# Macaron block with attention: the value product's four column groups become four quarters of the queries, one burst per key block

## The chip, the cores and the metric

The kernel runs on one core of one Trainium2 chip. The metric is the device time of one execution in microseconds. Engines: TensorE (PE), VectorE (DVE), ScalarE (ACT), GpSimd (POOL) and SyncE (SP), which issues all DMAs here.

## The reference

Input x is (4, 1024, 128) in f32. Three sublayers, each with a layernorm in front:

```
x = x + 0.5 * ffn(layernorm(x))      # 8 experts, top 2, hidden 256
x = x + attention(layernorm(x))      # 16 heads of 8, rotary, softmax over 1024 keys, out projection
x = x + 0.5 * ffn(layernorm(x))      # same weights as the first
```

With four batches and 16 heads there are 64 (batch, head) pairs, called heads 0 to 63 here. For each, attention computes softmax(q k / sqrt(8)) v for 1024 queries and 1024 keys. The key stack holds the f32 values split into bf16 parts, so the score product has 48 rows; three more rows subtract the maximum of each query.

## The kernel before

**Stages.** The first FFN takes chunks of 512 tokens (NCH = 8) and computes q, k and v behind them. Then come the 64 heads. The second FFN takes the 8 chunks again; each chunk's attention is normalised, projected and added one chunk ahead of it (`norm_attention`, `out_projection`, `add_attention`). PE, ACT, DVE, POOL and SP each run an instruction stream of their own, in program order, tied together by semaphores. Heads 4 to 59 are a hardware loop of 14 rounds of four heads, in which a wait's count comes from a register; heads 0 to 3 and 60 to 63 are written out.

**One head.** It has 8 key blocks of 128 keys. A score tile is 128 keys by 512 queries, so a head has 16 tiles (HALVES), i = 2 kb + j. Per i, PE issues in this order (`head`, L934):

- `key_scores` (L900, matmul L907): 51 rows, 512 columns, bf16, into one of three score banks (`score`, SCORE_BANKS = 3). It waits until the exp three places before has read that bank (`bank_free`). PE's place 7 in this rotation (MT_AT) is a transposition of the maxima of the next head (`max_transpose`, L897), which takes a bank for itself.
- `max_scores` (L869, matmul L878): 48 rows, for the head after the next; two of them make a tile of 128 queries by 1024 keys, on which DVE takes a maximum (L1252). Two such tiles are buffered. Q and K of heads two apart lie in different halves of the partitions.
- at every fourth i (3, 7, 11, 15), `weigh_values` (L910, matmul L921): the value product of a pair of key blocks, in f32, with the exponentials as the moving operand. Four matmuls fill four column groups of 32 in the array, hence four groups of 32 partitions of one PSUM bank (`opsum`): (even block, first 512 queries), (even, second), (odd, first), (odd, second). In the trace each of these matmuls is two, a first and a second pass. A value tile has 8 columns of v and columns of ones, which give the denominator. The pair weighed is the one before: at i = 3 the last pair of the previous head, at i = 7 the first of this one.

ACT does the 16 exponentials of a head (L675) into `probs`, 8 slots of 1024 columns. After exp 3 it copies the previous head's `opsum` to `ot` (`o_copy`, L657 to L663), and before exp 7 it copies the transposed maxima to `mrow` (L655). `weigh_values` of the first pair of a head waits for this `ot` (`ot_ready`). POOL splits the maxima into three bf16 parts and copies the head's values to `vh` (`v_head`). SP loads q and k of the head three further on, stores `ot` to the DRAM tensor `o_parts`, and loads `mrow` into Q (`head`, L381).

**After the heads.** `o_parts` holds, for each head and each half of the queries, two partial sums (even and odd key blocks). For a chunk SP loads both denominators (`load_den`), DVE adds and inverts them (`invert_denominator`), SP stores the result and loads both partial sums and the inverse, spread over the 8 rows of a head (`load_att`); POOL adds the two partial sums (`sum_attention`, L533), DVE multiplies (`norm_attention`, L1125).

Of the kernel before, what the change touches and what calls it, by code (L numbers as in the profile page):

```python
# [22 lines left out]
F32 = mybir.dt.float32  # L23
# [8 lines left out]
P = 128  # L32
# [22 lines left out]
HALF = 64  # L55
PAIRS = KB // 2
VW = 32
PIECE = H * CH // P
QSLOTS = 4
PSLOTS = 8  # L60
HALVES = 2 * KB
# [12 lines left out]
def at_least(eng, sem, count):  # L74

    if isinstance(count, int) and count <= 0:
        return
    eng.wait_ge(sem, count)  # L78
# [49 lines left out]
def build(nc, x_in, qkv_w, qkv_b, v_b, out_w, out_b, wr_t, w1_in, w2_t, cos_t, sin_t, out):  # L128
    q_stack = nc.dram_tensor("q_stack", (NH, STACK, T), BF16).ap()
    k_stack = nc.dram_tensor("k_stack", (NH, STACK, T), BF16).ap()  # L130
    rdens = nc.dram_tensor("rdens", (NCH, H, CH), F32).ap()
    o_parts = nc.dram_tensor("o_parts", (NH, P, CH), F32).ap()
    with ExitStack() as ctx:
        def sb(name, shape, dt=F32):
            return ctx.enter_context(nc.sbuf_tensor(name, shape, dt))

        def sem(name):
            return ctx.enter_context(nc.semaphore(name))
# [68 lines left out]
        mrow = sb("mrow", [PARTS * KB, 2, P], BF16)  # L207
        ot = sb("ot", [P, 2, CH])
        att = sb("att", [P, 2, 2, CH])
        att_sum = sb("att_sum", [P, CH])  # L210
        den = sb("den", [P, 2, PIECE])
        den_sum = sb("den_sum", [P, PIECE])
        rden_thin = sb("rden_thin", [P, PIECE])
# [18 lines left out]
        mpsum = ps[0:PARTS * KB, MT_BANK, 0:P // 2].bitcast(BF16)  # L232
        opsum = ps[:, 7, :]

# [58 lines left out]
        den_loaded = sem("den_loaded")  # L293
        den_summed = sem("den_summed")
        att_summed = sem("att_summed")
        den_inverted = sem("den_inverted")
# [17 lines left out]
        def _(sp):  # L314
# [34 lines left out]
            def load_head(r, u):  # L349
                n = QSLOTS * r + u  # L350

                at_least(sp, probs_used, PAIRS * (n - QSLOTS + 1))
                for tile, stack in ((Q, q_stack), (K, k_stack)):
                    sp.dma_start(tile[u][0:STACK, :],
                                 stack[bass.ds(n, 1)].rearrange("n s t -> (n s) t")).then_inc(head_loaded[u], 16)
# [36 lines left out]
            def load_den(r, u):  # L392
                c = CPB * r + u
                at_least(sp, den_inverted, c)
                for a in range(2):
                    src = o_parts[bass.ds(r * H, H), 32 * (2 * a + u) + HD, :].rearrange("h (s q) -> h s q", q=PIECE)
                    sp.dma_start(den[:, a, :], src).then_inc(den_loaded, 16)


            def load_att(r, u):  # L400
                c = CPB * r + u
                sp.wait_ge(den_inverted, c + 1)
                sp.dma_start(rdens[bass.ds(c, 1)].rearrange("c h (s q) -> (c h s) q", q=PIECE),
                             rden_thin[:]).then_inc(rden_stored, 16)

                at_least(sp, attn_ready, c - 1)
                alone(sp)
                sp.wait_ge(rden_stored, 16 * (c + 1))
                for a in range(2):
                    at = 32 * (2 * a + u)  # L410
                    sp.dma_start(att[:, u, a, :], o_parts[bass.ds(r * H, H), at:at + HD, :]).then_inc(att_loaded[u], 16)
                thin = rdens[bass.ds(c, 1)].rearrange("c h q -> (c h) q").unsqueeze(1).to_broadcast((H, HD, CH))
                sp.dma_start(rden[:, u, :], thin).then_inc(att_loaded[u], 16)

# [46 lines left out]
        def _(pool):  # L461
# [50 lines left out]
            def v_head(r, u):  # L512
                n = QSLOTS * r + u

                at_least(pool, probs_used, PAIRS * (n - 1))
                alone(pool)
                nc.gpsimd.tensor_copy(vh[:, u % 2, :, 0:HD],
                                      V[:].rearrange("p b h k d -> p (b h) k d")[:, bass.ds(n, 1), :, :]
                                      .rearrange("p n k d -> p (n k) d")).then_inc(vh_ready, 1)
# [8 lines left out]

            def sum_attention(r, u):
                c = CPB * r + u  # L530
                pool.wait_ge(att_loaded[u], 48 * (r + 1))
                at_least(pool, attn_ready, c)
                nc.gpsimd.tensor_tensor(att_sum[:], att[:, u, 0, :], att[:, u, 1, :], ALU.add).then_inc(att_summed, 1)  # L533

            for u in range(QSLOTS):
# [4 lines left out]
            for u in range(QSLOTS):  # L540
                head(NH // QSLOTS - 1, u)
                if u == 2:
                    sum_attention(0, 0)
            sum_attention(0, 1)
            with pool.Fori(1, NCH // CPB) as r:
                for u in range(CPB):
                    sum_attention(r, u)


        @block.scalar  # L550
        def _(sc):
# [105 lines left out]
            def o_copy(r, u):  # L657
                n = QSLOTS * r + u
                sc.wait_ge(probs_used, PAIRS * (n + 1))

                if not (isinstance(r, int) and r == 0 and u < 2):
                    sc.wait_ge(ot_stored[u % 2], 16 * (2 * r + u // 2))
                nc.scalar.activation(ot[:, u % 2, :], opsum, ACT.Copy).then_inc(ot_ready, 1)  # L663

            def head(r, u, more=True, first=False):
                n = QSLOTS * r + u
                for i in range(HALVES):
                    kb, j = i // 2, i % 2
                    if i == MT_AT and more:
                        mrow_copy(r + (u + 1) // QSLOTS, (u + 1) % QSLOTS)  # L670
                    sc.wait_ge(scores_in_psum, HALVES * n + i + 1)
                    if i % 4 == 0:

                        at_least(sc, probs_used, PAIRS * (n - 1) + i // 4 + 1)
                    nc.scalar.activation(probs[:, kb % PSLOTS, j * CH:(j + 1) * CH], score[i],  # L675
                                         ACT.Exp, scale=SCALE).then_inc(probs_ready, 1)
                    if i == 3 and not first:
                        o_copy(r + (u - 1) // QSLOTS, (u - 1) % QSLOTS)
                    if i == 5 and not more:
                        xT_copy(NCH, 0, early_t)  # L680
# [16 lines left out]
        def _(pe):  # L697
# [211 lines left out]

            def weigh_values(r, u, pair):  # L910


                n = QSLOTS * r + u
                pe.wait_ge(probs_ready, HALVES * n + 4 * pair + 4)
                if pair == 0:

                    at_least(pe, ot_ready, n)
                    pe.wait_ge(vh_ready, n + 1)
                for c in range(4):
                    kb, j = 2 * pair + c // 2, c % 2  # L920
                    last = nc.tensor.matmul(opsum[32 * c:32 * c + VW, :], vh[:, u % 2, kb, :],  # L921
                                            probs[:, kb % PSLOTS, j * CH:(j + 1) * CH],
                                            start=(pair == 0), stop=(pair == PAIRS - 1), skip_group_check=True)
                last.then_inc(probs_used, 1)
# [9 lines left out]
            def head(r, u, maxes=True, row=True, first=False, early=None):  # L934
                for i in range(HALVES):
# [4 lines left out]
                    if maxes:  # L940
                        max_scores(r + (u + 2) // QSLOTS, (u + 2) % QSLOTS, i)
                    if j == 1 and kb % 2 and kb >= 3:
                        weigh_values(r, u, kb // 2 - 1)
                    elif j == 1 and kb == 1 and not first:
                        weigh_values(r + (u - 1) // QSLOTS, (u - 1) % QSLOTS, PAIRS - 1)
                    if early == 0 and i == 5:
# [13 lines left out]
            for u in range(QSLOTS):  # L960
                head(NH // QSLOTS - 1, u, maxes=u < 2, row=u < 3, early=u - 2)
            weigh_values(NH // QSLOTS - 1, QSLOTS - 1, PAIRS - 1)
            pe.wait_ge(ot_ready, NH)
# [7 lines left out]
        def _(dve):  # L971
# [138 lines left out]
            def invert_denominator(c):  # L1110
                dve.wait_ge(den_loaded, 32 * (c + 1))
                nc.vector.tensor_tensor(den_sum[:], den[:, 0, :], den[:, 1, :], ALU.add).then_inc(den_summed, 1)
                dve.wait_ge(den_summed, c + 1)

                at_least(dve, rden_stored, 16 * c)
                alone(dve)
                nc.vector.reciprocal(rden_thin[:], den_sum[:]).then_inc(den_inverted, 1)

            def norm_attention(r, u):

                c = CPB * r + u
                dve.wait_ge(att_loaded[u], 48 * (r + 1))
                dve.wait_ge(att_summed, c + 1)
                at_least(dve, proj_in_psum, c)
                nc.vector.tensor_tensor(attn[:], att_sum[:], rden[:, u, :], ALU.mult).then_inc(attn_ready, 1)  # L1125

# [215 lines left out]
```

## Time and profile before

| | |
|---|---|
| three runs | 1371.33, 1371.33, 1372.31 us; median 1371.33 |
| the profiled execution's own time | 1371.65 us |
| its span | 1369.9 us |
| PE busy | 1254.1 us, 92% |
| DVE busy | 1134.6 us, 83% |
| ACT busy | 801.9 us, 59% |
| POOL busy | 153.7 us, 11% |
| mean granted clock of TensorE | 0.989 |
| exponentials, L675 | 1024, mean 601 ns |
| maxima, L1252 | 512, mean 1220 ns |
| key products, L907 | 1024, mean 384 ns |
| value product passes, L921 | 2048, mean 607 ns |

Times in the trace are in microseconds from the span's start. A matmul's record includes its way through the array, so the records of matmuls that follow one another overlap; the distance between their starts is the time that each costs. PEld is the loading of weights. A row's bracket says how long the engine sat idle just before, and which engine's work ended that.

### The profile page before, as it was taken

To read this page: it belongs to the slowest core of one execution; us is meant where nothing else is said; L and a number is where in the kernel's file an instruction comes from. 1 tells how busy PE (TensorE), PEld (TensorE's weight loads), DVE (VectorE), ACT (ScalarE), POOL (GpSimd) and SP (SyncE) were. 2 spreads that over 40 slices of the span, in tenths; PEclk is the share of its full clock that TensorE was granted. 3 is DMA by queue.
4 is the path that set the end of the run, shared out by engine and by line. 5 is a ranking of instruction groups with operands and counts; after the bars stand their busy time and mean duration, and the time that the engine had idled before them with its cause. 6 is when DMAs were issued, how large, how long until landed. Compare 5 with 4: busy or idle time off the path is not lost.

```text
span 1369.9 us, 27688 instructions
## 1 busy us (share of the span) xinstructions
PE 1254.1 (92%) x8192; PEld 596.7 (44%) x8192; DVE 1134.6 (83%) x2314; ACT 801.9 (59%) x1540; POOL 153.7 (11%) x458
## 2 busy tenths in 40 slices
PE   5999999999798888888888888888889899999998
PEld 3766666666312222222222222222222576767776
DVE  7877877788799999899988998899896687777775
ACT  4433333333268888888888888888888323333332
POOL 1022012221211111111111111111111000000000
PEclk9999999999879999999999999999999999999999
DMA  7010011110311111111111111111111211101100
GB/s 200 1 47 24 25 47 46 47 28 20 86 44 55 42 41 41 54 41 41 41 54 41 41 41 54 41 41 41 50 49 49 61 35 34 35 14 29 32 1 16
DMA packets 52135, 59.19 MB, mean 43 GB/s; under 512 B 10977, under 2 KB 33377, under 8 KB 52065
## 3 DMA queue, kind: packets, MB, share of 16 engines
q1 hardware_dynamic: 52064, 58.36, 14.2%
q8 instruction: 31, 0.51, 0.2%
q14 instruction: 40, 0.32, 0.1%
HBM read 26.22 MB, written 31.72 MB: 42 GB/s over the span
## 4 chain that ended last, share of the span: by engine, by line
PE 74%; ACT 12%; DVE 6%; issue 6%; DMA 1%; ACTq 1%; DVEq 0%; SPq 0%
PE ps L779 21%; PE ps L921 19%; PE ps L766 14%; PE ps L907 14%; ACT probs L675 12%; PE ps L736 2%; DVE X L1106 1%; PE ps L756 1%; DVE act L1094 1%; PE ps L700 1%; DVE mx L1252 1%; ACTq L78 1%; PE ps L743 1%; PE ps L773 0%; PE ps L878 0%
## 5 line engine op out<-in xcount | busy, mean ns | idle before, releaser
L1252 DVE TENSOR_REDUCE mx<-ps 128x1 f32<-128x1024 f32 x512 | 608.3, 1220 | 65.0 <-PE ps L878 44.8
L675 ACT ACTIVATE probs<-ps 128x512 f32<-128x512 f32 x1024 | 534.5, 601 | 106.9 <-PE ps L907 106.9
L907 PE MATMUL ps<-Q,K 51*128 51x512 bf16 x1024 | 310.9, 384 | 55.4 <-ACT probs L675 55.2
L604 ACT ACTIVATE sg<-ps,unscale 128x512 f32<-128x512 f32 x256 | 173.8, 687 | 312.1 <-PE ps L779 276.3
L878 PE MATMUL ps<-K,Q 48*128 48x512 bf16 x1008 | 339.7, 389 | 4.6 <-DVE mx L1252 3.6
L921 PE MATMUL ps<-probs,vh 128*32 128x512 f32 x2048 | 273.9, 607 | 0.1
L766 PEld LDWEIGHTS ps<-w,act 128*128 128x128 f32 x2048 | 247.9, 192 | 17.1
L766 PE MATMUL ps<-w,act 128*128 128x128 f32 x2048 | 249.0, 275 | 0.0
L907 PEld LDWEIGHTS ps<-Q,K 51*128 51x128 bf16 x1024 | 80.3, 93 | 362.4 <-ACT probs L675 328.2
L1094 DVE SCALAR_TENSOR_TENSOR act<-ps,unscale,sg 128x512 f32<-128x512 f32 x256 | 183.1, 744 | 58.5 <-PE ps L779 17.9
L779 PE MATMUL ps<-x_hi,w_hi 128*128 128x512 f16 x512 | 194.7, 380 | 13.2 <-DVE act L1094 8.5
L779 PE MATMUL ps<-x_hi,w_lo 128*128 128x512 f16 x512 | 194.5, 380 | 0.0
L779 PE MATMUL ps<-x_lo,w_hi 128*128 128x512 f16 x512 | 194.5, 380 | 0.0
L1106 DVE SCALAR_TENSOR_TENSOR X<-ps,rw,X 128x128 f32<-128x128 f32 (+1 forms) x512 | 144.1, 343 | 57.8 <-PE ps L766 57.2
L878 PEld LDWEIGHTS ps<-K,Q 48*128 48x128 bf16 x1008 | 79.0, 93 | 72.5 <-DVE mx L1252 65.5
L779 PEld LDWEIGHTS ps<-x_hi,w_hi 128*128 128x128 f16 x512 | 51.6, 101 | 69.0 <-DVE act L1094 16.7
L779 PEld LDWEIGHTS ps<-x_hi,w_lo 128*128 128x128 f16 x512 | 50.1, 98 | 60.8 <-issue 0.7
L504 POOL TENSOR_SCALAR negm<-mx 128x8 f32<-128x8 f32 x64 | 15.1, 236 | 521.3 <-DVE mx L1252 521.3
L779 PEld LDWEIGHTS ps<-x_lo,w_hi 128*128 128x128 f16 x512 | 50.2, 98 | 48.5 <-issue 4.9
L921 PEld LDWEIGHTS ps<-probs,vh 128*32 128x32 f32 x2048 | 40.4, 108 | 59.3 <-issue 57.9
L483 POOL TENSOR_TENSOR qf<-rot 128x512 f32<-128x512 f32 x16 | 20.4, 1275 | 258.5 <-DVE rot L1141 258.5
L663 ACT ACTIVATE ot<-ps 128x512 f32<-128x512 f32 x64 | 38.2, 597 | 7.2 <-PE ps L921 1.1
(86 smaller groups left out, 605.1 us busy)
## 6 DMA issues: line engine op xcount, KB each, us to landing
o_parts<-ot SPq DMA_DIRECT2D x64, 256.0 KB, 2.2
q_stack<-parts SPq DMA_DIRECT2D x48, 128.0 KB, 2.3
k_stack<-parts SPq DMA_DIRECT2D x48, 128.0 KB, 2.3
Q<-q_stack SPq DMA_DIRECT2D x64, 96.0 KB, 2.3
K<-k_stack SPq DMA_DIRECT2D x64, 96.0 KB, 2.3
att<-o_parts SPq DMA_DIRECT2D x16, 256.0 KB, 3.6
probs<-w_in SPq DMA_DIRECT2D x8, 256.0 KB, 5.0
rden<-rdens SPq DMA_DIRECT2D x8, 256.0 KB, 4.2
```

The costliest lines, as they stand in the source:

```text
L604: nc.scalar.activation(sg[:, j, :], hid[2 * j], ACT.Silu, scale=unscale[:, e, 2 + j:3 + j]).then_inc(silu_done, 1)
L663: nc.scalar.activation(ot[:, u % 2, :], opsum, ACT.Copy).then_inc(ot_ready, 1)
L675: nc.scalar.activation(probs[:, kb % PSLOTS, j * CH:(j + 1) * CH], score[i], ACT.Exp, scale=SCALE).then_inc(probs_ready, 1)
L736: last = nc.tensor.matmul(bank, wqkv[:, 2 * w + i, :], x2T[:], start=True, stop=True)
L766: last = nc.tensor.matmul(ypsum[s][:, t, :], act[:, s, j, t * P:(t + 1) * P], w2[:, e, j, :], start=(j == 0), stop=(j == 1))
L779: last = nc.tensor.matmul(bank, w[:, e, at:at + P], x[:, k, :], start=(n == 0), stop=(n == 2))
L878: last = nc.tensor.matmul(maxps[t % 2][:, half, :], Q[u][0:STACK, t * P:(t + 1) * P], K[u][0:STACK, half * CH:(half + 1) * CH], start=True ...
L907: nc.tensor.matmul(score[i], K[u][0:ROWS, kb * P:(kb + 1) * P], Q[u][0:ROWS, j * CH:(j + 1) * CH], start=True, stop=True).then_inc(scores_ ...
L921: last = nc.tensor.matmul(opsum[32 * c:32 * c + VW, :], vh[:, u % 2, kb, :], probs[:, kb % PSLOTS, j * CH:(j + 1) * CH], start=(pair == 0) ...
L1094: nc.vector.scalar_tensor_tensor(out=act[:, e % 2, j, :], in0=hid[2 * j + 1], scalar=unscale[:, e, j:j + 1], in1=sg[:, j, :], op0=ALU.mult ...
L1106: last = nc.vector.scalar_tensor_tensor(out=xt, in0=ypsum[e % 2][:, t, :], scalar=rw[:, k, t, e:e + 1], in1=xt, op0=ALU.mult, op1=ALU.add)
L1252: nc.vector.tensor_reduce(mx[:, u % 2, t:t + 1], pair.rearrange("p a b -> p (a b)"), AX_X, ALU.max).then_inc(max_read, 1)
```

## The change

The four column groups of the value product now hold the four quarters of 256 queries (QW = 256) of a single key block. There is one burst per key block, at every second i, for the block two before it (LAG = 2): at i = 1 and 3 the last two of the previous head, at i = 5 the first of this one. Each column group holds a complete sum, so nothing is added afterwards: `sum_attention` on POOL and the addition of denominators on DVE are gone, `opsum`, `ot` and `o_parts` are 256 columns wide, and `att` and `rden` are loaded by quarters (four DMAs for a chunk where there were three). `o_copy` follows exp 4. The counts of `probs_used` are doubled, and exps with j = 0 wait for it.

```diff
-PAIRS = KB // 2
+QUARTERS = 4
+QW = T // QUARTERS
+LAG = 2
...
-    rdens = nc.dram_tensor("rdens", (NCH, H, CH), F32).ap()
-    o_parts = nc.dram_tensor("o_parts", (NH, P, CH), F32).ap()
+    rdens = nc.dram_tensor("rdens", (NCH, 2, H, QW), F32).ap()
+    o_parts = nc.dram_tensor("o_parts", (NH, P, QW), F32).ap()
...
-        ot = sb("ot", [P, 2, CH])
-        att = sb("att", [P, 2, 2, CH])
-        att_sum = sb("att_sum", [P, CH])
-        den = sb("den", [P, 2, PIECE])
-        den_sum = sb("den_sum", [P, PIECE])
+        ot = sb("ot", [P, 2, QW])
+        att = sb("att", [P, 2, CH])
+        den = sb("den", [P, PIECE])
...
-        opsum = ps[:, 7, :]
+        opsum = ps[:, 7, 0:QW]
...
-                at_least(sp, probs_used, PAIRS * (n - QSLOTS + 1))
+                at_least(sp, probs_used, KB * (n - QSLOTS + 1))
...
                 for a in range(2):
-                    src = o_parts[bass.ds(r * H, H), 32 * (2 * a + u) + HD, :].rearrange("h (s q) -> h s q", q=PIECE)
-                    sp.dma_start(den[:, a, :], src).then_inc(den_loaded, 16)
+                    src = o_parts[bass.ds(r * H, H), VW * (2 * u + a) + HD, :].rearrange("h (s q) -> h s q", q=PIECE)
+                    sp.dma_start(den[a * HALF:(a + 1) * HALF, :], src).then_inc(den_loaded, 16)
...
                 for a in range(2):
-                    at = 32 * (2 * a + u)
-                    sp.dma_start(att[:, u, a, :], o_parts[bass.ds(r * H, H), at:at + HD, :]).then_inc(att_loaded[u], 16)
-                thin = rdens[bass.ds(c, 1)].rearrange("c h q -> (c h) q").unsqueeze(1).to_broadcast((H, HD, CH))
-                sp.dma_start(rden[:, u, :], thin).then_inc(att_loaded[u], 16)
+                    at = P // QUARTERS * (2 * u + a)
+                    sp.dma_start(att[:, u, a * QW:(a + 1) * QW], o_parts[bass.ds(r * H, H), at:at + HD, :]).then_inc(att_loaded[u], 16)
+                    thin = rdens[bass.ds(c, 1), a].rearrange("c h q -> (c h) q").unsqueeze(1).to_broadcast((H, HD, QW))
+                    sp.dma_start(rden[:, u, a * QW:(a + 1) * QW], thin).then_inc(att_loaded[u], 16)
...
-                at_least(pool, probs_used, PAIRS * (n - 1))
+                at_least(pool, probs_used, KB * (n - 1))
...
-            def sum_attention(r, u):
-                c = CPB * r + u
-                pool.wait_ge(att_loaded[u], 48 * (r + 1))
-                at_least(pool, attn_ready, c)
-                nc.gpsimd.tensor_tensor(att_sum[:], att[:, u, 0, :], att[:, u, 1, :], ALU.add).then_inc(att_summed, 1)
...
-                sc.wait_ge(probs_used, PAIRS * (n + 1))
+                sc.wait_ge(probs_used, KB * (n + 1))
...
-                    if i % 4 == 0:
-
-                        at_least(sc, probs_used, PAIRS * (n - 1) + i // 4 + 1)
+                    if j == 0:
+
+                        at_least(sc, probs_used, KB * (n - 1) + kb + 1)
...
-                    if i == 3 and not first:
+                    if i == 4 and not first:
                         o_copy(r + (u - 1) // QSLOTS, (u - 1) % QSLOTS)
...
-            def weigh_values(r, u, pair):
+            def weigh_values(r, u, kb):
...
-                pe.wait_ge(probs_ready, HALVES * n + 4 * pair + 4)
-                if pair == 0:
+                pe.wait_ge(probs_ready, HALVES * n + 2 * kb + 2)
+                if kb == 0:
...
-                for c in range(4):
-                    kb, j = 2 * pair + c // 2, c % 2
-                    last = nc.tensor.matmul(opsum[32 * c:32 * c + VW, :], vh[:, u % 2, kb, :],
-                                            probs[:, kb % PSLOTS, j * CH:(j + 1) * CH],
-                                            start=(pair == 0), stop=(pair == PAIRS - 1), skip_group_check=True)
+                for c in range(QUARTERS):
+                    last = nc.tensor.matmul(opsum[VW * c:VW * (c + 1), :], vh[:, u % 2, kb, :],
+                                            probs[:, kb % PSLOTS, c * QW:(c + 1) * QW],
+                                            start=(kb == 0), stop=(kb == KB - 1), skip_group_check=True)
...
-                    if j == 1 and kb % 2 and kb >= 3:
-                        weigh_values(r, u, kb // 2 - 1)
-                    elif j == 1 and kb == 1 and not first:
-                        weigh_values(r + (u - 1) // QSLOTS, (u - 1) % QSLOTS, PAIRS - 1)
+                    if j == 1 and kb >= LAG:
+                        weigh_values(r, u, kb - LAG)
+                    elif j == 1 and not first:
+                        weigh_values(r + (u - 1) // QSLOTS, (u - 1) % QSLOTS, KB + kb - LAG)
...
-            weigh_values(NH // QSLOTS - 1, QSLOTS - 1, PAIRS - 1)
+            for kb in range(KB - LAG, KB):
+                weigh_values(NH // QSLOTS - 1, QSLOTS - 1, kb)
...
-                nc.vector.tensor_tensor(den_sum[:], den[:, 0, :], den[:, 1, :], ALU.add).then_inc(den_summed, 1)
-                dve.wait_ge(den_summed, c + 1)
...
-                nc.vector.reciprocal(rden_thin[:], den_sum[:]).then_inc(den_inverted, 1)
+                nc.vector.reciprocal(rden_thin[:], den[:]).then_inc(den_inverted, 1)
...
-                dve.wait_ge(att_loaded[u], 48 * (r + 1))
-                dve.wait_ge(att_summed, c + 1)
+                dve.wait_ge(att_loaded[u], 64 * (r + 1))
...
-                nc.vector.tensor_tensor(attn[:], att_sum[:], rden[:, u, :], ALU.mult).then_inc(attn_ready, 1)
+                nc.vector.tensor_tensor(attn[:], att[:, u, :], rden[:, u, :], ALU.mult).then_inc(attn_ready, 1)
```

## Rows read from the trace of the kernel before

**Rows 1.** The head of the page: the span of the profiled execution.

```profile
span 1369.9 us, 27688 instructions
```

**Rows 2.** Busy time by stretch: the loop of heads; columns engine, busy us, (instructions), PEclk, DMA share.

```profile
431.00:1021.00 590.00, 519.93 (x3628) 132.13 (x3627) 530.91 (x448) 494.54 (x1006) 69.42 (x332) 1.00 0.13 44
```

**Rows 3.** Timeline of DVE and PEld in one head: start, length, engine, line, operation.

```profile
708.98 1.23 DVE L1252 TENSOR_REDUCE mx<-ps 128x1 f32<-128x1024 f32 x1 [0.31 <-PE ps L878]
...
710.12 1.22 DVE L1252 TENSOR_REDUCE mx<-ps 128x1 f32<-128x1024 f32 x1
...
711.39 0.09 PEld L878 LDWEIGHTS ps<-K,Q 48*128 48x128 bf16 x1 [0.29 <-DVE mx L1252]
```

**Rows 4.** Chain of waits, one pair of key blocks in a head.

```profile
708.81 0.61 ACT probs L675
...
709.46 0.39 PE ps L907
...
709.85 1.00 PE ps L921 x8
...
711.28 0.61 ACT probs L675
```

**Rows 5.** Timeline of ACT, from exps 0 to 3 to exp 8 of one head.

```profile
703.25 2.06 ACT L675 ACTIVATE probs<-ps 128x512 f32<-128x512 f32 x4 [0.41 <-PE ps L907]
705.36 0.60 ACT L663 ACTIVATE ot<-ps 128x512 f32<-128x512 f32 x1
705.85 1.57 ACT L675 ACTIVATE probs<-ps 128x512 f32<-128x512 f32 x3
707.29 0.26 ACT L655 ACTIVATE mrow<-ps 24x128 bf16<-24x128 bf16 x1
...
708.81 2.06 ACT L675 ACTIVATE probs<-ps 128x512 f32<-128x512 f32 x4 [0.79 <-PE ps L907]
```

**Rows 6.** Timeline of ACT: the copies of heads 0, 3 and 59.

```profile
399.64 0.60 ACT L663 ACTIVATE ot<-ps 128x512 f32<-128x512 f32 x1
...
430.61 0.60 ACT L663 ACTIVATE ot<-ps 128x512 f32<-128x512 f32 x1
...
1022.29 0.60 ACT L663 ACTIVATE ot<-ps 128x512 f32<-128x512 f32 x1
```

**Rows 7.** Timeline of PE around one burst of value products.

```profile
701.43 0.39 PE L907 MATMUL ps<-Q,K 51*128 51x512 bf16 x1 [0.15 <-ACT probs L675]
...
701.75 1.06 PE L921 MATMUL ps<-probs,vh 128*32 128x512 f32 x8
...
702.21 0.61 PE L921 MATMUL ps<-probs,vh 128*32 128x512 f32 x4
...
702.75 0.39 PE L907 MATMUL ps<-Q,K 51*128 51x512 bf16 x1
...
702.98 0.38 PE L907 MATMUL ps<-Q,K 51*128 51x512 bf16 x1
```

**Rows 8.** Timeline of PE in the second FFN: 16 f32 passes of 128 columns.

```profile
1110.15 1.95 PE L766 MATMUL ps<-w,act 128*128 128x128 f32 x16
1111.94 0.38 PE L779 MATMUL ps<-x_hi,w_hi 128*128 128x512 f16 x1
```

**Rows 9.** Timeline of PE in head 62: key products 6 and 7, a transposition between them.

```profile
1044.30 0.39 PE L907 MATMUL ps<-Q,K 51*128 51x512 bf16 x1
...
1044.78 0.39 PE L907 MATMUL ps<-Q,K 51*128 51x512 bf16 x1
```

**Rows 10.** Chain of waits: end of the heads and first chunk after them.

```profile
1062.48 1.11 PE ps L921 x8
...
1075.03 1.42 issue
```

**Rows 11.** Timeline of SP's issues and of DVE in the same chunk.

```profile
1069.42 1.27 SPq L411 DMA_DIRECT2D att<-o_parts  x2
...
1077.46 0.55 DVE L1117 RECIPROCAL rden_thin<-den_sum 128x64 f32<-128x64 f32 x1 [0.17 <-DVE den_sum L1112]
```

More of the change, by code:

```diff
@@ L293, in build @@
         den_loaded = sem("den_loaded")
-        den_summed = sem("den_summed")
-        att_summed = sem("att_summed")
         den_inverted = sem("den_inverted")
@@ L402, in load_att @@
                 sp.wait_ge(den_inverted, c + 1)
-                sp.dma_start(rdens[bass.ds(c, 1)].rearrange("c h (s q) -> (c h s) q", q=PIECE),
+                sp.dma_start(rdens[bass.ds(c, 1)].rearrange("c a h (s q) -> (c a h s) q", q=PIECE),
                              rden_thin[:]).then_inc(rden_stored, 16)
@@ L541, in _ @@
                 head(NH // QSLOTS - 1, u)
[L542 to L547, printed above, removed]
         @block.scalar
```

## The prediction, made before the kernel was run

> **What bounds the kernel now.** I read the page first, then busy time by stretch, the chain of waits, and the timelines of single engines inside one head. The profiled execution took 1371.65 us, of which its span is 1369.9 us [rows 1]; the median of the three runs is 1371.33 us, 0.3 us less. A measurement of this kernel can tell about 0.2% from no change, 2.7 us. The change sits in the attention stage, heads 0 to 63, about 384 to 1064 us. In its loop VectorE (DVE) looks like the bound, 90% busy against 88% for TensorE (PE) and 84% for ScalarE (ACT) [rows 2]. The timelines say otherwise. Two reductions that find their data ready start 1.14 us apart (708.98, 710.12), so two key blocks need 2.28 us of DVE [rows 3]. Two key blocks take 2.47 us (the exp at 708.81 and the one at 711.28), and the chain of waits shows what the 2.47 is made of: exp (0.61), key product, the burst of value products, key product, next exp [rows 4]. There are only three score banks, so key product i waits for exp i-3. After the key product and its partner of the max scores, PE's queue holds the burst for 1.00 us (709.85), and until it is through, no score reaches ACT. ACT then idles 0.41 us per pair and 0.79 us once a head [rows 4, 5]. So the loop is a handshake between PE and ACT, lengthened by a burst that comes in one piece. A head takes (1022.29 - 430.61)/56 = 10.566 us [rows 6]. The reader is to see in rows 4 that the idle time of ACT is the burst's length, not a lack of PE time.
>
> **The pieces, measured.** With K for the key product (the max product M starts with it, in other rows of the array):
> - K to next K after a burst: 0.23 us (702.75, 702.98). K to burst: 0.32 us (701.43, 701.75), which is 0.10 more than K to K. First pass to second pass: 0.46 us (701.75, 702.21). Second pass to next K: 0.54 us (702.21, 702.75) [rows 7]. An f32 pass streams at two array cycles a column, 0.427 us for 512 columns at 2.4 GHz; 16 passes of 128 columns take 1.79 us, 0.112 each, where this rate gives 0.107 [rows 8]. So a burst is 2 x 0.427 streaming plus about 0.03 between passes plus 0.12 before the next K: 0.145 us fixed.
> - K start to its exp: 0.50 us (702.75, 703.25) [rows 5, 7]. Exp start to the K that it frees: 0.65 us (708.81, 709.46) [rows 4]. Exp to the following activation: 0.49 us (705.36, 705.85) [rows 5].
> - Reduction to the max product that it frees: 0.05 us after its end, 710.12 + 1.22 to 711.39 [rows 3].
>
> **The change, part by part.**
> 1. *Burst.* Four column groups still run at once, and each pass has 256 columns: 0.213 us. The number of passes per burst stays two, so I keep the fixed part: 2 x 0.213 + 0.145 = 0.57 us. The trace has no 256-column burst. Bounds: 0.50 us (half of 1.00, nothing fixed), and 0.79 us, if each pass held up the next for all that its record (0.61) has beyond streaming: 2 x (0.213 + 0.18) [rows 7]. I take 0.57, since rows 8 show passes of 128 columns, shorter still, 0.112 us apart: short passes overlap their ends.
> 2. *Steady key block.* K, K, burst: 0.23 + 0.32 + 0.57 = 1.115 us (unrounded pieces), 2.23 per pair where it was 2.47. PE is in this order by itself; check the others: exp i-3 for K is free after 0.50 + 0.49 + 0.65 = 1.64 us, against 2.23 from K to the K four later; odd ones 1.15 against 1.34. ACT needs 0.97. The wait for probs_used, now at every even exp, lies within the 0.50, which was read at an exp that has it. DVE needs 1.14 per tile, 0.025 more than PE, which it makes good at the head's stall below. So the handshake disappears, and PE's own order sets the pace.
> 3. *A new wait.* The copy of the previous head's output (L663) moves behind exp 4, and the first burst of this head, which must wait for that copy, moves from place 7 up to place 5. Before, the copy followed exp 3 and was done long before place 7. Now, from K4: exp 4 at 0.50, copy at 0.99, copy done and PE released at 0.99 + 0.37 + 0.05 = 1.41, burst 0.57, K6 at 1.98 us, where a steady key block takes 1.115: a stall of 0.86 us per head. Behind the waiting burst on PE stand K6, K7, M6, M7 and the transposition; ACT (exp 6) and DVE (tile 3) wait for these. The copy itself has 256 columns, which no row has. The same engine takes 0.26 us at 128 and 0.60 us at 512 columns [rows 5]; these are the bounds, and I take the line between, 0.37.
>    The Trainium skill ("ScalarE: Activation LUTs", Rules for kernel authors) budgets about 0.3 us per activation and 0.83 ns per element. For 512 that is 0.72 us where the trace has 0.60, and for 256 it is 0.51: by it each head would be 0.14 us longer and the gain about 9 us smaller.
> 4. *Transposition at place 7.* K6 to K7 with it, nothing late: 0.48 us (1044.30, 1044.78) [rows 9]. K6 to K8 = 0.48 + 0.32 + 0.57 = 1.37 us. The exp that K7 needs (exp 5, right behind the copy) is done at 1.24 + 0.65 = 1.89 from K4, K7 comes at 2.46; exp 6 and the mrow copy are also done in time (1.15 and 1.30 against 1.37 and 1.60 after K6). The wait for ACT that stood here is covered by the stall of step 3, at no more cost.
> 5. *Head.* Six key blocks at 1.115, one at 1.98, one at 1.37: 10.04 us against 10.566. Saved 0.53 us x 56 = 29.5 us. Heads 1 to 3, outside the loop, took 10.32 us each (399.64 to 430.61) [rows 6] and get about 0.36 shorter, the last four about 0.3: 2.3 us. Head 0 runs in part at the 1.2 GHz level and has no copy to wait for; four more switches cost it 0.8 us.
> 6. *End of the stage.* Last burst 1.11 + copy 0.60 become about 0.57 + 0.37: 0.8 us saved [rows 10]. Then rden lands at 1075.03 and attn starts 1.42 us later, because POOL's addition stands between [rows 10]. The addition goes, but SP issues a fourth DMA first (0.64 us each, 1.27 for two [rows 11]): 0.8 us. With the addition of denominators, 0.3 us with the wait behind it [rows 11], 1.1 us. In later chunks of the second FFN the removed work lies beside PE, which has no idle time there; costed at nothing; if PE were to wait for DVE it would be 0.3 us each.
> 7. *DMA and POOL in the stage.* The store of o has half the bytes, the counts of probs_used are doubled with the same meaning, SP's order is the same. mrow is loaded 4.2 us after K6 at the latest; next K0 comes at 5.8: covered, with 1.6 us to spare. vh is copied a head ahead.
>
> Sum: 29.5 + 2.3 - 0.8 + 0.8 + 1.1 = 32.9; 1371.65 - 32.9 = 1338.8, say **1339 us**.
>
> **Rivals.**
> - *The burst is dearer than 0.57 and the kernel gets slower.* The mechanism: twice as many bursts, each with 8 loads and 8 matmuls, so PE must take in 24 load and matmul records per key block. The fastest sustained rate in the trace is 16 loads and 16 matmuls in 1.79 us, 56 ns a record [rows 8]. If that is a limit of taking in instructions and not only of streaming, a key block needs 24 x 56 ns = 1.34 us, a head at least 10.75: 60 x 0.18 = 11 us slower, **1382 us**, and up to 1395 where stalls are not made up. It decides from a burst of 0.64 us (0.53/8 above mine). For it: nothing in the trace has such short bursts. Against it: eight loads of a burst start 7 ns apart, and streaming alone explains rows 8. Its far bound, 0.79 us per burst, would give a head of 11.8 and 1443 us. Chance 0.18. The same side has a rule of the Trainium skill ("TensorEngine Tiling (Array Packing)", Key Properties): a change of tiling mode drains the engine. By that rule the number of drains doubles; rows 7 have it as 0.10 and 0.12 us, and they are in my 0.57, so it alone does not turn the sign.
> - *The gain is larger.* The fixed part shrinks (burst 0.50): head 6 x 1.04 + 1.91 + 1.30 = 9.47, **1305 us**. Chance 0.16 for 1300 to 1325. If in addition the wait for the copy were hidden, DVE would be the bound at 8 x 1.14 = 9.1 us: 1285 us, chance 0.02; against it stand the orders of both queues.
> - *The new wait eats more.* A copy at its upper bound of 0.60 costs 0.23 us a head, 14 us in all (1353); a burst of 0.60 to 0.63 costs 8 x 0.03 to 0.06 us a head, 14 to 29 us: 1353 to 1368 us. Chance 0.12.
> - *It cancels*, within 0.2%: stall and doubled switches are together what the handshake had cost. Chance 0.04.
>
> **How the numbers follow.** My forecast (1325 to 1353) has 0.48. Faster by over 0.2%: 0.48 + 0.16 + 0.02 + 0.12 = 0.78; within: 0.04; slower: 0.18. The range leaves out the far ends of the burst's bounds, which rows 8 speak against: 1306 (burst 0.50) to 1382 (56 ns per record).
>
> **What the profile after would show.** Bursts of 8 records with the next K 0.57 us after the burst's start; K0 of one key block to K0 of the next 1.11 to 1.12 us; a head 10.0 us; ot 0.37 us long, and PE waiting for it (ACT ot as releaser of L921's idle time) some 60 times, 0.8 to 0.9 us each; the reductions with one gap per head in the place of two and the pairs' small gaps. Step 1 is wrong if the next K comes at 0.64 or later; step 3 if PE does not wait for ot, or K4 to K6 is not near 1.98. The forecast falls if DVE runs without gaps (larger gain), or if PE's records in steady key blocks lie more than 1.18 us apart.

## The result and the profile after

The changed kernel takes 1360.32 us (median of four runs, 1358.65 to 1362.02) against 1371.33 us: a ratio of 0.9915, 95% interval 0.9899 to 0.9931. It is faster, by 11 us, where 33 us had been forecast. The profiled execution took 1362.02 us, the longest of the four, with a span of 1360.2 us.

The page after, its head and the groups that answer to the table of before (columns: line, engine, operation, shapes, count, busy us, mean ns, idle time before):

```profile
span 1360.2 us, 32042 instructions
PE 1269.9 (93%) x10240; PEld 615.2 (45%) x10240; DVE 1112.3 (82%) x2306; ACT 816.2 (60%) x1540; POOL 142.5 (10%) x450
...
L661 ACT ACTIVATE probs<-ps 128x512 f32<-128x512 f32 x1024 | 568.5, 594 | 93.0 <-PE ps L893 74.0
L906 PE MATMUL ps<-probs,vh 128*32 128x256 f32 x4096 | 329.6, 393 | 56.0 <-ACT probs L661 42.0
```

In this kernel L893 is the key product, L864 the max product, L906 the burst of value products, L661 the exp, L649 the copy to ot. PE has 16 us more busy time (1269.9 against 1254.1), and still the time fell: what PE stands idle went from 116 to 90 us.

The timeline of PE after, one head and the start of the stall (it answers to [rows 7] and [rows 9]):

```profile
702.17 0.39 PE L893 MATMUL ps<-Q,K 51*128 51x512 bf16 x1
702.37 0.38 PE L864 MATMUL ps<-K,Q 48*128 48x512 bf16 x1
702.66 0.39 PE L893 MATMUL ps<-Q,K 51*128 51x512 bf16 x1
...
704.65 0.39 PE L893 MATMUL ps<-Q,K 51*128 51x512 bf16 x1
...
706.13 0.64 PE L906 MATMUL ps<-probs,vh 128*32 128x256 f32 x8 [0.87 <-ACT probs L661]
706.70 0.39 PE L893 MATMUL ps<-Q,K 51*128 51x512 bf16 x1
...
707.18 0.39 PE L893 MATMUL ps<-Q,K 51*128 51x512 bf16 x1
...
709.18 0.39 PE L893 MATMUL ps<-Q,K 51*128 51x512 bf16 x1
...
710.28 0.39 PE L893 MATMUL ps<-Q,K 51*128 51x512 bf16 x1
```

702.17 is K0, 702.66 K1, 704.65 K4, 706.70 K6, 707.18 K7, and 709.18 and 710.28 are K10 and K12. A burst is 0.57 us to the next K (706.13, 706.70), a steady key block 1.10 us (709.18 to 710.28; 1.107 on the mean of the loop), K6 to K7 0.48 us: each as forecast. K4 to K6 is 2.05 us (forecast 1.98); in the first head of each round of the loop it is 2.18. New to the forecast is the head's first line: K0 to K1 is 0.49 us, where 0.23 was expected.

The copies in ACT's timeline (heads 3 and 59, [rows 6]; then head 63) and one stall of ACT and of DVE:

```profile
434.97 0.38 ACT L649 ACTIVATE ot<-ps 128x256 f32<-128x256 f32 x1
...
1017.75 0.38 ACT L649 ACTIVATE ot<-ps 128x256 f32<-128x256 f32 x1
...
1059.01 0.38 ACT L649 ACTIVATE ot<-ps 128x256 f32<-128x256 f32 x1 [0.67 <-PE ps L906]
```

```profile
705.65 0.38 ACT L649 ACTIVATE ot<-ps 128x256 f32<-128x256 f32 x1
705.91 0.61 ACT L661 ACTIVATE probs<-ps 128x512 f32<-128x512 f32 x1
707.20 0.60 ACT L661 ACTIVATE probs<-ps 128x512 f32<-128x512 f32 x1 [0.68 <-PE ps L893]
```

```profile
707.63 9.34 DVE L1235 TENSOR_REDUCE mx<-ps 128x1 f32<-128x1024 f32 x8 [1.03 <-PE ps L864]
```

The copy takes 0.38 us (forecast 0.37). It ends at 706.03 (705.65 + 0.38), and the burst starts 0.10 us later. The burst's bracket names the exponentials, but the exp that was running then ends only at 706.52, and the two that this burst reads were done by 703.76; what it waited for is the copy. The profile has such a wait before the burst 63 times, once a head: 49 put down to an exp, 14 to `ot`. DVE has one gap per head, of 1.03 us, in the place of two of 0.3 to 0.4 and the small ones. A head takes (1017.75 - 434.97)/56 = 10.407 us, against 10.566 before and 10.04 in the forecast.

By parts, from the two profiled executions (span to span, -9.7 us): up to the copy of head 3, +4.4 us (434.97 against 430.61); 56 heads, -8.9; the last four, -0.1; from the last copy to the end, -5.1 (1360.2 - 1059.01 = 301.2 against 306.3).

### The profile page after: what moved, and what is told of

The parts are those of the page before. It is cut to its first block, busy times and chain, and to the rows that moved or that the text cites. A ratio compares the mean times of both kernels' runs of the same rounds, so it can differ in the third digit from the quotient of the medians.

```text
span 1360.2 us, 32042 instructions
## 1 busy us (share of the span) xinstructions
PE 1269.9 (93%) x10240; PEld 615.2 (45%) x10240; DVE 1112.3 (82%) x2306; ACT 816.2 (60%) x1540; POOL 142.5 (10%) x450
## 4 chain that ended last, share of the span: by engine, by line
PE 82%; ACT 6%; issue 6%; DVE 4%; SPq 1%; ACTq 0%; DMA 0%; DVEq 0%
PE ps L765 22%; PE ps L906 19%; PE ps L893 18%; PE ps L752 15%; ACT probs L661 5%; PE ps L722 2%; PE ps L864 1%; DVE X L1092 1%; PE ps L742 1%; PE ps L686 1%; PE ps L883 1%; PE ps L729 1%; DVE act L1080 1%; PE ps L759 1%; SPq L320 0%
## 5 line engine op out<-in xcount | busy, mean ns | idle before, releaser
L1235 DVE TENSOR_REDUCE mx<-ps 128x1 f32<-128x1024 f32 x512 | 591.9, 1217 | 75.1 <-PE ps L864 69.4
L661 ACT ACTIVATE probs<-ps 128x512 f32<-128x512 f32 x1024 | 568.5, 594 | 93.0 <-PE ps L893 74.0
L906 PE MATMUL ps<-probs,vh 128*32 128x256 f32 x4096 | 329.6, 393 | 56.0 <-ACT probs L661 42.0
L893 PE MATMUL ps<-Q,K 51*128 51x512 bf16 x1024 | 333.2, 386 | 0.5 <-ACT probs L661 0.2
L864 PE MATMUL ps<-K,Q 48*128 48x512 bf16 x1008 | 328.1, 390 | 2.5 <-DVE mx L1235 2.0
L906 PEld LDWEIGHTS ps<-probs,vh 128*32 128x32 f32 x4096 | 82.4, 108 | 247.2 <-ACT probs L661 193.6
L893 PEld LDWEIGHTS ps<-Q,K 51*128 51x128 bf16 x1024 | 72.5, 93 | 234.5 <-ACT probs L661 226.2
L864 PEld LDWEIGHTS ps<-K,Q 48*128 48x128 bf16 x1008 | 71.6, 93 | 13.5 <-DVE mx L1235 8.9
L580 ACT ACTIVATE tanh_gap<-gap 128x4 f32<-128x4 f32 x16 | 3.3, 205 | 52.5 <-DVE gap L1049 52.5
```

The costliest lines, as they stand in the source:

```text
L864: last = nc.tensor.matmul(maxps[t % 2][:, half, :], Q[u][0:STACK, t * P:(t + 1) * P], K[u][0:STACK, half * CH:(half + 1) * CH], start=True ...
L893: nc.tensor.matmul(score[i], K[u][0:ROWS, kb * P:(kb + 1) * P], Q[u][0:ROWS, j * CH:(j + 1) * CH], start=True, stop=True).then_inc(scores_ ...
L906: last = nc.tensor.matmul(opsum[VW * c:VW * (c + 1), :], vh[:, u % 2, kb, :], probs[:, kb % PSLOTS, c * QW:(c + 1) * QW], start=(kb == 0), ...
L1235: nc.vector.tensor_reduce(mx[:, u % 2, t:t + 1], pair.rearrange("p a b -> p (a b)"), AX_X, ALU.max).then_inc(max_read, 1)
```

## The experiments

Loop time per head is read in each profile as in [rows 6].

**1. The unused place of the bank rotation.** The first suspicion fell on K0 to K1. A head has 16 scores and one transposition, 17 places, in a rotation of 18 that must be a multiple of three banks; place 17 is empty. So K1, in place 1, takes the bank of place 16, K15, and the order is K15, K0, K1: a distance of two, not three. K0 takes the bank of K14 in the same way. The exps of that moment:

```profile
711.89 0.60 ACT L661 ACTIVATE probs<-ps 128x512 f32<-128x512 f32 x1
...
712.38 0.59 ACT L661 ACTIVATE probs<-ps 128x512 f32<-128x512 f32 x1
```

and the weight loads of K0 and K1, which follow (timeline of PEld):

```profile
712.54 0.09 PEld L893 LDWEIGHTS ps<-Q,K 51*128 51x128 bf16 x1 [0.46 <-ACT probs L661]
...
713.03 0.09 PEld L893 LDWEIGHTS ps<-Q,K 51*128 51x128 bf16 x1 [0.30 <-ACT probs L661]
```

Exp 14 starts at 711.89 and K0 0.65 us later; exp 15 at 712.38 and K1 0.65 us later, the same 0.65 as in [rows 4]. So both products come as soon as their bank is read. The experiment moves the empty place to where PE stands still anyway.

```diff
-SCORE_PLACE = [i + (i >= MT_AT) for i in range(HALVES)]
-MT_BANK = MT_AT % SCORE_BANKS
+GAP_AT = 6
+MT_PLACE = 8
+SCORE_PLACE = [i + (i >= GAP_AT) + (i >= MT_AT) for i in range(HALVES)]
+MT_BANK = MT_PLACE % SCORE_BANKS
...
-    if before == PLACES - 1 or (before == MT_AT and not row):
+    if before == GAP_AT or (before == MT_PLACE and not row):
...
-    if before == MT_AT:
+    if before == MT_PLACE:
...
-                    bank_free(n - 1, MT_AT, True)
+                    bank_free(n - 1, MT_PLACE, True)
```

> The changed kernel with the unused place of the bank rotation moved from the end of the head (place 17) to just before key product 6, where PE stands still anyway for the copy of the outputs. Theory P (places): with place 17 unused, key products 0 and 1 of a head come only two places after the scores whose banks they take, so K1 waits for exp 15 of the head before; that costs 0.31 us a head. With the gap moved, K0 to K1 falls from 0.49 to 0.23 us, a head from 10.37 to 10.06 us, the time from 1360 to about 1342 us. Rival Q: the delay at a head's start is PE's own work there (register operations and separate waits for mrow and for the loaded q and k): then K0 to K1 stays at 0.4 to 0.5 us and the time at 1360. Rival D: it is the wait for DVE's maxima: also 1360.

Measured: 1339.99 us, ratio to the kernel before 0.9758 (0.9741 to 0.9774); 10.086 us per head. K0 to K1 in its timeline of PE:

```profile
699.66 0.39 PE L895 MATMUL ps<-Q,K 51*128 51x512 bf16 x1
699.89 0.38 PE L895 MATMUL ps<-Q,K 51*128 51x512 bf16 x1
```

0.23 us. PE's own work at the head's start and the waits for DVE's maxima are coded the same in both kernels, so P stands and Q and D fall: 0.32 us a head, 20 us in all, hung on the wait for exps 14 and 15, the second above all.

**2. The copy one exp earlier.**

```diff
-                    if i == 4 and not first:
+                    if i == 3 and not first:
```

> The changed kernel with the copy of the previous head's output after exp 3 again, in the place of after exp 4. Theory W (the new wait): the first burst of a head waits for that copy, and K4 to K6 goes from 2.05 to about 1.42 us (copy 0.37 after K4, 0.38 long, 0.10 to PE, burst 0.57), 0.6 us less a head, 1360 to about 1324 us. Rival: ACT or DVE takes over at once (exp 4 now sits behind the copy), at most 0.3 us a head, 1342 us.

Measured: 1324.6 us, ratio 0.9648 (0.963 to 0.9667); 9.790 us per head. The stall in its timeline of PE (K4, burst, K6) and the copy:

```profile
702.01 0.39 PE L893 MATMUL ps<-Q,K 51*128 51x512 bf16 x1
...
703.00 0.64 PE L906 MATMUL ps<-probs,vh 128*32 128x256 f32 x8 [0.39 <-ACT ot L649]
703.58 0.39 PE L893 MATMUL ps<-Q,K 51*128 51x512 bf16 x1
```

```profile
702.38 0.39 ACT L649 ACTIVATE ot<-ps 128x256 f32<-128x256 f32 x1
```

The copy starts 0.37 us after K4, as expected; K4 to K6 here is 1.57 us, because PE went on 0.23 us after the copy's end and not 0.10. But this is the first head of a round of the loop, which was the slower one (2.18 us) in the changed kernel too. The head behind it has the 0.10 (copy from 712.27 to 712.66) and 1.43 us, where 1.42 was expected:

```profile
711.91 0.39 PE L893 MATMUL ps<-Q,K 51*128 51x512 bf16 x1
...
712.76 0.64 PE L906 MATMUL ps<-probs,vh 128*32 128x256 f32 x8 [0.25 <-issue]
713.34 0.39 PE L893 MATMUL ps<-Q,K 51*128 51x512 bf16 x1
```

Like with like, both kinds of head lose 0.62 us between K4 and K6 (2.05 to 1.43, 2.18 to 1.56), and that is the whole difference of a head. In all the copy's place was worth 36 us, and moving one line takes it back; 0.32 us of the wait, beyond a steady block's 1.11, is still there.

**3. Both.**

> Both edits of the two runs before. If P and W are both right and independent: 10.37 - 0.31 - 0.63 = 9.43 us a head, about 1304 us. If DVE's reductions (8 x 1.16 us = 9.3) already bound the head with one of them, the sum of the two gains is not reached: 1312 us or more.

Measured: 1305.51 us, ratio 0.9504 (0.9488 to 0.9521); 9.500 us per head. The two losses are independent but for 0.03 us: 10.407 - 0.321 - 0.617 = 9.47. The 0.03 stand at K6 to K8, 1.41 us in three of four heads where 1.37 is PE's own order: the moved place begins to cost there (experiment 6). DVE does not bound yet; it has a gap of 0.34 us per head.

**4. Bursts in pairs.** Quarters and no additions, but two bursts in a row after i = 3, 7, 11, 15.

```diff
-                    if j == 1 and kb >= LAG:
-                        weigh_values(r, u, kb - LAG)
-                    elif j == 1 and not first:
-                        weigh_values(r + (u - 1) // QSLOTS, (u - 1) % QSLOTS, KB + kb - LAG)
+                    if j == 1 and kb % 2 and kb >= 3:
+                        for b in (kb - 3, kb - 2):
+                            weigh_values(r, u, b)
+                    elif j == 1 and kb == 1 and not first:
+                        for b in (KB - 2, KB - 1):
+                            weigh_values(r + (u - 1) // QSLOTS, (u - 1) % QSLOTS, b)
```

> The changed kernel (quarters, nothing added afterwards, half the bytes) with its bursts issued two at a time after every fourth key product, as the kernel before issued its one. Theory H (the handshake): the gain comes from the shorter wait of the next key product; two bursts in a row take about 1.07 us, exp to exp over a pair becomes 0.65 + 0.32 + 1.07 + 0.50 = 2.54 us, a head about 10.9, the time about 1385 to 1392 us, slower than the kernel before. Rival: the gain comes from the removed additions and the smaller transfers: then it stays at about 1360 us.

Measured: 1375.66 us, ratio 1.0023 (1.0013 to 1.0032); 10.675 us per head. Its chain of waits:

```profile
703.25 0.61 ACT probs L661
...
703.91 0.39 PE ps L893
...
704.29 1.00 PE ps L906 x16
705.30 0.33 PE ps L893
...
705.73 0.61 ACT probs L661
```

The handshake is back, link for link as in [rows 4], 2.48 us per pair. So the gain of the change comes from the shorter piece in which PE's queue holds the burst, and the rival falls. The size was off: two bursts in a row take 1.00 us and not 1.07, as much as the one burst of before. Sixteen passes of 256 columns cost no more than eight of 512; the fixed part, 0.15 us, is paid once per burst in one piece and does not grow with the number of passes. From the last copy to the end this kernel takes 1373.5 - 1072.11 = 301.4 us, like the changed one: the 5 us there belong to the removed additions and the smaller transfers.

**5. The empty place alone, in the kernel before.** The edit of experiment 1.

> The kernel before, with nothing but the unused place of the bank rotation moved to just before key product 6. Theory P says that there the two-place distance at a head's start costs nothing, since the 1.00 us burst after K15 covers exp 15, and that the place is harmful or neutral where it goes: within 3 us of 1371 us. Rival: the move is a gain by itself, in whichever kernel, of the 18 to 20 us that it gave to the changed one: 1352 us.

Measured: 1383.72 us, ratio 1.0078 (1.0064 to 1.0092), 10.722 us per head. It is slower, by 11 us, where no more than 3 was expected: the rival falls clearly, but "harmful or neutral" was harmful. That there was nothing to gain at the head's start fits P. The loss of 0.16 us a head is found in its trace, between K4 and K8 (on the mean of the loop 3.30 us against 3.15). The distance of two now lies at K6, which waits for exp 4, and at the transposition, which waits for exp 5; and before exp 4 ACT has the copy to `ot`. K6:

```profile
700.58 0.39 PE L909 MATMUL ps<-Q,K 51*128 51x512 bf16 x1 [0.76 <-ACT probs L677]
```

Exp 4 starts at 699.93 and K6 0.65 us later. K5 to K6 is 1.11 us on the mean, where the kernel before had 0.22; K6 to K7 gives most of it back, 0.65 for 1.39.

**6. Bursts three key blocks behind, copy after exp 5, empty place moved.** The edit of experiment 1, and:

```diff
-LAG = 2
+LAG = 3
...
-                    if i == 4 and not first:
+                    if i == 5 and not first:
```

> The changed kernel with the gap moved, bursts three key blocks behind (LAG = 3) and the copy after exp 5. Theory W: nothing waits for the copy any more (about 0.3 us a head are left of that stall in the run with both edits); PE's order is then 8 x 1.11 + 0.26 = 9.15 us a head, and DVE's reductions at 1.14 to 1.16 us each, 9.1 to 9.3, become the bound: about 1290 us, with PE waiting for DVE's maxima. Rival: the stall only moves on (copy of exp 5 reaches the burst at place 7 late): 1300 to 1306 us.

Measured: 1295.26 us, ratio 0.9439 (0.9425 to 0.9454); 9.331 us per head. Busy time of its loop, columns as in [rows 2]:

```profile
431.00:950.00 519.00, 517.97 (x5405) 144.01 (x5403) 508.66 (x447) 498.80 (x1001) 69.79 (x333) 1.00 0.12 36
```

The stall for the copy is gone. PE's records cover 99.8% of the time, but they overlap, so a share of busy time hides short waits. Six blocks of 1.107 us, K4 to K6 at the same, and K6 to K8 at 1.37 would be 9.12 us; the head takes 0.21 more. The rest stands where the empty place now is:

```profile
708.78 0.09 PEld L895 LDWEIGHTS ps<-Q,K 51*128 51x128 bf16 x1 [0.46 <-ACT probs L663]
...
709.26 0.09 PEld L885 LDWEIGHTS ps<-identb,mparts 128*24 128x24 bf16 x1 [0.31 <-ACT probs L663]
```

```profile
709.42 0.39 PE L895 MATMUL ps<-Q,K 51*128 51x512 bf16 x1
```

K6 (708.78) starts 0.65 us after exp 4 (708.13), the transposition 0.65 after exp 5. K6 to K7 is 0.64 us and not 0.48, and K4 to K6 1.15 and not 1.11. So moving the empty place made the distance of two cheaper, not free: 0.32 us a head at the head's start, 0.21 here. DVE, busy 98%, was expected to bound and does not: it has one gap of 0.19 us per head. The time lies between the two that were expected (1290 and 1300 to 1306). This is the best version measured, 76 us ahead of the kernel before and 65 ahead of the change as made.

## Why the prediction was right or wrong

The direction held; the size did not, 11 us where 33 were forecast. The measured 1360.32 us lies outside the forecast's 1325 to 1353. It falls in the band of a rival, "the new wait eats more" (1353 to 1368), by chance: neither of its causes came about, as the copy took 0.38 us and not 0.60, and the burst 0.57 and not 0.60 to 0.63.

- *Step 1, the burst*: right, 0.57 us. The rival that the burst is dearer, 24 records at 56 ns, fell: a key block with 24 records took 1.11 us, 46 ns each.
- *Step 2, the steady key block*: right in size, 1.11 us, and wrong in scope. **This is the step that failed**: "check the others: exp i-3 for K is free". The three-places rule was taken for the whole head. At a head's start it is two places, and there the handshake between PE and ACT still sets the pace: K1 comes 0.65 us after the start of exp 15. With the step's own pieces, K1 is free 1.64 us after K14 and due after 1.34: 0.30 us a head that the sum lacks. Before, the burst of 1.00 us behind K15 had just covered that: exp 15 started at 702.23, so K1 was free at 702.88, and it came at 702.98 [rows 7]. The same shortening that brought the gain laid it bare. Experiment 1 puts it at 0.32 us a head, 18 us over the 56 heads of the loop, of the 20.5 us by which the loop missed (56 x (10.407 - 10.04)). The unused place stands in the code (`PLACES = 18`, and `before == PLACES - 1` in `place_before`), and was not costed.
- *Step 3, the new wait*: right. K4 to K6 took 2.05 us where 1.98 was forecast, and 2.18 in one head of four; most of the 0.07 is that PE went on 0.10 us after the copy's end and not 0.05. This is 5.5 us over the loop; steady key blocks of 1.107 us for 1.115 give about 3 back, and so the loop's miss is made up. Experiment 2 shows that the wait stood where it was said to stand. Its 36 us were in the forecast already, so it is not why the gain was small, but it is what the change gave away.
- The estimate by the Trainium skill ("ScalarE: Activation LUTs", Rules for kernel authors), 0.51 us for a copy of 256 columns, was too long: the trace has 0.378 us, and the line between two rows gave 0.37. The rule's 0.3 us is for an activation whose bias is an operand of one value per partition, and this copy has no such bias.
- *Step 4*: right, 0.48 us.
- *Step 5, the ends of the stage*: up to the copy of head 3 the kernel was 4.4 us later where it was to be 0.3 us earlier. The profiled execution stayed longer at the lower of the clock's two levels there: the rows below, after and then before, have 0.91 against 1.00 from 395 us. In the profile of experiment 1 the same stretch has 1.00, and its copy of head 3 starts at 430.48, 4.5 us sooner; about 1 us of that is the moved place. The fastest run of the changed kernel, with a mean clock of 0.989 against 0.984, took 1358.65 us, 3.4 less than the profiled one. So some 3.5 of the 4.7 us by which the start missed belong to this execution. The last four heads gained 0.1 us and not 1.2; that was not looked into.

```profile
395.00:431.00 36.00, 33.63 (x323) 8.27 (x327) 30.25 (x27) 29.64 (x59) 3.74 (x18) 0.91 0.10 29
```

```profile
395.20:431.00 35.80, 33.36 (x231) 8.20 (x227) 33.22 (x28) 31.05 (x63) 5.03 (x24) 1.00 0.12 40
```

- *Step 6, after the heads*: right in kind, too small: 5.1 us from the last copy to the end where 1.1 was forecast. The transfers of half the size also landed sooner, rden 2.5 us after its issue where it had been 4.2, att 2.6 and not 3.6, which the forecast did not count; and in the first chunk PE's idle time before the out projection went. Before, in the timeline of PE, and after, in the chain of waits:

```profile
1077.20 1.16 PE L773 MATMUL ps<-wo,attn 128*128 128x128 f32 x8 [1.43 <-DVE attn L1125]
```

```profile
1069.18 1.78 PE ps L752 x16
1070.96 0.89 PE ps L759 x8
1071.86 2.59 PE ps L765 x12
```

In the changed kernel the out projection (L759) follows the expert's product with no wait between. Measured from the last copy it comes 1.8 us sooner, 0.2 of which is the shorter copy; by the end of the first chunk PE is 3.8 us ahead. The other 1.3 us come in later chunks, 0.25 to 0.45 at a time. The step had costed these at nothing, with 0.3 us each if PE were to wait for DVE; the sizes fit that, but the waits themselves were not looked at.

Sum against the forecast, in the profiled executions: 20.5 (loop) + 4.7 (start) + 1.9 (last four heads and last copy) - 4.0 (after the heads) = 23.1; forecast 1338.8, measured 1362.02.

## What to carry to other kernels

When two engines hand a few buffers to and fro, count the distance between a buffer's use and its reuse at every position of the order, at the seams of the loop too, before shortening what lies between: what covered the tight spot may be just what is shortened. A large block on an in-order queue costs its length at every handshake behind it, and splitting it helps even where the total work grows. When an output copy moves, write down where its reader now stands; here one line (the copy after exp 3) was worth three times the change itself. And read waits from the starts of an engine's instructions, not from its share of busy time: in experiment 6 a share of 99.8% hid 0.21 us a head.

## What the runs showed that was not expected

- Sixteen f32 passes of 256 columns in four column groups took 1.00 us in one piece, the same as eight of 512 (experiment 4, [rows 4]); one group of eight took 0.57 us. The overhead beyond streaming, 0.15 us beside the 0.10 on the way in, is the same for eight and for sixteen passes, so it comes with the change between key products and burst: three steps from pass to pass cost no more than one. The Trainium skill ("TensorEngine Tiling (Array Packing)", Key Properties) says that a change of tiling mode drains the engine; the trace agrees in that the time is lost at the changes, 0.10 and 0.15 us, but does not show what the engine does in it.
- In experiment 6 PE was busy 517.97 of 519 us while a head took 9.33 us: DVE with 8 reductions of 1.14 us fits beside it with 0.19 us to spare. An estimate from these rows: without the 0.21 us at the empty place PE's order would take 9.12 us, and DVE's reductions need 8 x 1.14 = 9.12 as well, so a further gain would need both shortened. No run tried it.
